# Products of constants in the waits of TensorE, in a twelve-sublayer decoder on one core

## The reference, cut to what matters

```python
x = _layernorm(x + sublayer(x, ...), axis=-1)
```

```python
logits = jnp.einsum('bqhd,bkhd->bhqk', q, k) * scale
w = jax.nn.softmax(logits, axis=-1)
attn = jnp.einsum('bhqk,bkhd->bqhd', w, v).reshape(b, n, H * HD)
return attn @ Wout + bout
```

## Time and profile before

| | us |
|---|---|
| median of three timed executions | 1999.76 |
| the profiled execution, its own time | 2003.11 |
| its span from first to last instruction | 2001.3 |
| TensorE matmul busy | 1604.5 (80%) |
| VectorE busy | 1437.1 (72%) |
| TensorE weight load busy | 1193.9 (60%) |
| ScalarE busy | 777.8 (39%) |
| GpSimd busy | 522.6 (26%) |
| mean granted TensorE clock | 0.870 of full |

### The profile page before, as it was taken

The page is one execution under the profiler, slowest core; times in us unless marked ns, Lnnn a source line. Parts: engine busy times, 40 slices in busy tenths (PEclk is TensorE's granted clock), DMA queues, the critical chain, the costliest instruction groups (busy, mean ns, idle before and its releaser), DMA issues. The chain is left out here.

```text
span 2001.3 us, 31707 instructions
## 1 busy us (share of the span) xinstructions
PE 1604.5 (80%) x11439; PEld 1193.9 (60%) x11470; DVE 1437.1 (72%) x2398; ACT 777.8 (39%) x1231; POOL 522.6 (26%) x588
## 2 busy tenths in 40 slices
PE   4899999999868987266748568899995997888863
PEld 4678888887854663022446434588774885645631
DVE  3299999998645844899578573556774995657698
ACT  2367777675231532233324321433342002425532
POOL 1233333332412401377213002310000330414200
PEclk8999999999977986587878768999996998798985
DMA  3000000000000000000100001000001220010000
GB/s 143 23 28 29 26 26 26 26 26 1 1 11 13 2 7 34 0 0 0 45 3 2 27 37 72 2 25 11 12 21 42 74 73 27 4 56 2 2 0 21
DMA packets 17854, 49.20 MB, mean 25 GB/s; under 512 B 2003, under 2 KB 8276, under 8 KB 16470
## 3 DMA queue, kind: packets, MB, share of 16 engines
q1 hardware_dynamic: 17750, 47.78, 7.0%
HBM read 46.73 MB, written 1.05 MB: 24 GB/s over the span
## 5 line engine op out<-in xcount | busy, mean ns | idle before, releaser
L2146 DVE SCALAR_TENSOR_TENSOR arena<-psum,arena 128x1016 f32<-128x1016 f32 (+2 forms) x240 | 303.6, 1265 | 35.8 <-ACT arena L2083 30.1
L883 DVE TENSOR_REDUCE limits<-psum 128x4 f32<-128x512 f32 (+2 forms) x256 | 148.3, 620 | 91.9 <-PE psum L743 56.7
L1992 PE MATMUL psum<-ssm_XT_hi,ssm_split 128*128 128x512 f32 x640 | 195.1, 407 | 11.2 <-POOL ssm_split L1951 5.5
L851 ACT ACTIVATE PT<-psum 128x1024 f32<-128x1024 f32 x112 | 108.6, 1022 | 122.2 <-PE psum L774 122.2
L743 PE MATMUL psum<-K,QR 32*128 32x256 f32 (+1 forms) x320 | 125.1, 476 | 27.3 <-POOL K L719 16.5
L1992 PEld LDWEIGHTS psum<-ssm_XT_hi,ssm_split 128*128 128x128 f32 x640 | 116.3, 191 | 36.6 <-POOL ssm_split L1951 10.4
L2083 ACT ACTIVATE arena<-psum,arena 128x1024 f32<-128x1024 f32 x80 | 89.2, 1115 | 106.1 <-PE psum L1992 104.7
L2511 PE MATMUL psum<-expert,x 128*128 128x256 f16 x1024 | 114.2, 276 | 16.6 <-POOL expert L2497 16.6
L2649 POOL TENSOR_TENSOR fed<-dtx,b_all 128x1024 f32<-128x1024 f32 x32 | 103.2, 3245 | 77.8 <-ACT b_all L2698 44.4
L2511 PEld LDWEIGHTS psum<-expert,x 128*128 128x128 f16 x1024 | 101.3, 99 | 29.4 <-issue 16.7
L2524 DVE SCALAR_TENSOR_TENSOR acc<-psum,gate_now,acc 128x256 f32<-128x256 f32 x256 | 111.2, 483 | 8.5 <-PE psum L2511 7.7
(11 more groups left out here) (435 smaller groups left out, 3828.4 us busy)
## 6 DMA issues: line engine op xcount, KB each, us to landing
expert_mask<-in_expert_masks SPq DMA_DIRECT2D x32, 256.0 KB, 2.6
arena<-in_ssm_in SPq DMA_DIRECT2D x16, 384.0 KB, 2.9
arena<-in_L_xattn SPq DMA_DIRECT2D x1, 5120.0 KB, 16.0
arena<-in_ssm_in SPq DMA_DIRECT2D x16, 256.0 KB, 3.0
arena<-in_L_ffn SPq DMA_DIRECT2D x1, 2592.0 KB, 10.1
arena<-in_L_xattn SPq DMA_DIRECT2D x2, 1280.0 KB, 7.8
arena<-in_L_attn SPq DMA_DIRECT2D x1, 2272.0 KB
arena<-in_L_ffn SPq DMA_DIRECT2D x1, 2176.0 KB, 8.2
```

The costliest lines, as they stand in the source:

```text
L851: nc.scalar.activation(PT[:, u % 2, 2 * k:2 * k + 2, :, :].rearrange("p r h q -> p (r h q)"), p.psum[:, (2 + 2 * k) * 512:(4 + 2 * k) * 51 ...
L883: ins = nc.vector.tensor_reduce(limits[:, u % 2, r, :, k], score_bank(r)[:, :].rearrange("p (h k) -> p h k", h=4)[:, :, lo:hi], AX.X, ALU. ...
L1992: ins = nc.tensor.matmul(bank[tile_bank(r, tile) + half][:, :], w_part(tile, kw, c), x_part(kx, c, slice(half * 512, (half + 1) * 512)), s ...
L2146: ins = nc.vector.scalar_tensor_tensor(out[:, :, ago:], product[:, :, :P - ago], tap, out[:, :, ago:], ALU.mult, ALU.add)
```

## The change

A helper issues a number of products of the two constants, 128 x 512 each, with no wait before them and no reader behind them. In `attend` it is called ahead of scores 0 and 2 of the first unit and behind score 3 (6, 4 and 7 products, into bank 7). In `epilogue`, where there is no product, it is called ahead of each `turn_x` (6, 3, 3 and 2 products, into bank 0).

```diff
+def hold_clock(p, bank, times):
+
+    for _ in range(times):
+        p.nc.tensor.matmul(bank[:, :], p.c16("ident"), p.c16("after_row"), start=True, stop=True)
...
             def turn_x(j):
+                if added is None:
+                    hold_clock(p, bank[0], (6, 3, 3, 2)[j])
                 for b, ready in ((2 * j, s.x_ready), (2 * j + 1, s.x_odd_ready)):
                     pe.wait_ge(ready.sem, ready.at(j))
...
             for r in range(4):
+                if r % 2 == 0:
+                    hold_clock(p, bank[7], (6, 0, 4)[r])
                 score(0, r)
+            hold_clock(p, bank[7], 7)
             pe.wait_ge(s.loaded.sem, s.loaded.at(15))
             for u in range(U + 2):
```

## The result

The changed kernel took 1972.68 us (median of 4, 1971.30 to 1974.68) against 2000.80 for the kernel before beside it: ratio 0.9859, 95% interval 0.9842 to 0.9876, about 28 us faster. I had forecast 1986 in a range of 1975 to 1998. The direction held, and so did the clock as its cause. The size did not: the saving is twice the forecast, near rival (c), in which the clock holds through heads and ends and to which I had given 0.11.

The account below looks back on a forecast made before the run. The prediction took latency to bound the kernel: TensorE waits at sublayer ends and attention heads, then runs at half clock. Heads 6.1 + ends 8.0 = 14.1 us, so 1999.8 - 14.1 = 1985.7, say 1986 us, range 1975 to 1998.

Parts of the forecast that it names:

- rival (c): Heads and ends: the clock holds through both, 31.2 us saved, hence 1969 us, 1965 to 1977; chance 0.11.
- The prices: Each added 128x512 product costs 0.216 us at full clock, 0.427 at half; all 155 cost 33 or 66 us.
- the fit: Attention heads at full clock: 6 products take 1.3 of 1.8 us, 4 take 0.86 of 0.92, 7 take 1.5 over 1.39.
- The bounds: Most that could be saved: 18.9 us at the attention heads, 13.2 us at the sublayer ends.
- with 0.3 to 0.6 us lost: Ends with a low clock: it should rise amid the transposes, well before the next block, at this small loss.
- 8.0 us of 13.2: Five ends together: 0.4, 1.3, 1.5, 2.4 and 2.4 us, 8.0 in all, between -10.5 and 13.2.
- In the light attentions the fall is put off to the first unit, not taken away: Attention heads: nothing is added inside the loop, so the clock falls in the first unit; the first attention saves 0.8 of 5.5 us.
- 6.1 us of 18.9: Five attention heads together: 0.8 - 0.9 + 4.5 + 1.4 + 0.3 = 6.1 us, between -4 and 18.9.
- The second attention: Its head: added products late at half clock, 3.1 us in all; saving -0.9 us, between -3.1 and 0.
- (a): Ends stay at half clock, added products cost 2.1 us per end; 2004.2 us, slower; chance 0.08.
- (b): Ends pay 8.0 us, heads nothing, as the clock falls in the first unit; 1992 us, 1989 to 1996; chance 0.25.
- (d): Gains and delays cancel, or head gains are lost when the clock falls later; 1997 to 2001 us; chance 0.10.

Follow-up runs that it names:

- thin: The changed kernel with all 155 added products 32 columns wide instead of 512, timed beside the kernel before: 1997.75 us, ratio 0.9976.
- double numbers: The changed kernel with every number of added products doubled, timed beside the kernel before: 1995.52 us, ratio 0.9968.
- those between: Against the kernel before, only the 3, 3 and 2 products ahead of the later transposes in each of five ends: 1989.08 us, ratio 0.9931.
- ends: The changed kernel without the added products in `attend`, so only 14 in each of five ends, against the kernel before: 1985.40 us, ratio 0.9918.
- first six: Against the kernel before, only the 6 products ahead of the first transposes in each of five ends: 1995.13 us, ratio 0.9971.

## Why the prediction was wrong

The prices and the fit were right. An added product adds 0.216 us at full clock and 0.427 at half, 6, 4 and 7 fit at full clock, and from one group of transposes to the next it is 0.87 us with two products between and 1.74 with six, as the prices say. The bounds were nearly right: the ends gave 13.7 us in the profile for a bound of 13.2. What failed were the shares that I took of the bounds, in two steps. The first is the larger and the surer.

**"L0_attn, L1_ffn and L2_ffn ... with 0.3 to 0.6 us lost", and 8.0 us of 13.2.** The ends were undersized: 13.7 us in the profile (2.7, 2.1, 2.1, 3.8, 3.0 for 0.4, 1.3, 1.5, 2.4, 2.4), 14.1 in the second, 10.8 in the profile of the ends alone, and 16 us timed with the ends alone. The 5.7 us that were missing had three sources.

- 1.2 us: at L1_ffn and L2_ffn the clock was low and came back by the second or third group, as forecast, but the loss that I took off is given back in full, since the rounds at full clock, 0.44 + 0.65 = 1.09 us by the prices, are shorter than VectorE's (1.51) and catch up.
- 2.3 us: at L0_attn the clock did not fall, though TensorE idled 2.26 us ahead of the block, 1.12 behind the six and 2.49 behind the transposes. My reason for 0.4, the DMA wait behind the end, came true in the profile of the ends alone (0.1 us) and not in the two of the changed kernel.
- 2.2 us: at L1_attn and L2_xattn I had expected a full clock and still took 1.3 and 2.4 of bounds of 2.1 and 3.8. The prediction gives no reason for that, and there was none: they paid 2.1 and 3.8.

**"In the light attentions the fall is put off to the first unit, not taken away", "the later units as before", and 6.1 us of 18.9.** The fall is put off, but how far differs between two executions of the same kernel. In the first profile of the changed kernel the clock falls at 643.2, in the third unit of the first attention, and in the second at 633.6, at the start of the second unit:

```profile
632.50:643.20 10.70, 8.12 (x118) 5.29 (x119) 8.14 (x14) 5.05 (x8) 6.20 (x7) 1.00 0.01 2
643.23:646.64 3.41, 3.41 (x44) 2.31 (x38) 2.21 (x6) 1.94 (x2) 0.00 (x0) 0.50 0.02 5
```

```profile
629.85:633.60 3.75, 2.51 (x29) 1.48 (x29) 2.93 (x6) 1.79 (x3) 1.81 (x2) 1.00 0.00 0
633.64:647.26 13.62, 13.11 (x128) 9.07 (x128) 7.58 (x14) 5.52 (x10) 4.39 (x5) 0.50 0.01 2
```

It is 3.4 us at 0.50 in the one and 13.6 in the other, where the kernel before had 23.9, from 629.6 to 653.5. The other profiles show the same. In the first and fifth attention, of all kernels without products in the loop, six falls that begin in the third unit last 3.4 us each, six in the second 10.2 to 13.7, and two in the first 13.7. All told these two attentions are at 0.50 for 13.7 to 23.9 us in the kernels without the seven (or with thin ones) and for 3.4 to 13.7 in those with them. I had priced a later fall like an earlier one. Why a late one is short is not shown: that TensorE has no pauses at half clock (3.41 busy of 3.41) can't be all of it, since it is busy for 13.11 of 13.62 us in the long one too.

So the sizes scatter. Four first units of the first attention gave 3.9 us in the first profile and 1.3 in the second for a forecast of 0.8, those of the fifth 2.9 and 0.8 for 0.3 (part of which is not the change's, see below), three of the fourth 2.4 and 1.8 for 1.4, two of the third 4.4 in both for 4.5. The first and the fifth in the second profile:

```profile
629.85:651.55 21.70, 1.08 (x4) 0.38 (x4) 0.69 0.01 2
1775.80:1796.90 21.10, 1.00 (x4) 0.35 (x4) 0.68 0.01 2
```

The third, where the argument was from heavy units, was right, though not with unit 0 "nearly all at half clock": it was at 0.50 for 6.8 of its 10.1 us. Timed, the heads alone brought 15 us, 3 more or less, for 6.1; by the profiles, without what is not the change's, it is 10 and 8.5.

**The second attention.** The added products are late there, as forecast, but by less: 1.6 us from the first score to the first turn of limits, from the comparison with the kernel without, where I had 0.8 + 1.6 = 2.4. For the whole +1.2 us in one profile and -0.5 in the other stand against a forecast of +0.9, so the sign stays open, and so does whether leaving it out helps.

**The rivals.** (a), the half clock that costs more than it gives, fails even in the kernel with nothing ahead of the first transposes, where the clock is low at the start of every end. Late products cost more than a few tenths of a microsecond only at double numbers, and there at full clock. (b), heads that pay nothing, is what the six and the four alone do. (c) is nearest in the time: it took the bounds whole. But the clock did not hold through the first units. (d) is ruled out.

The Trainium skill's rule that a transpose does not count for the clock ("TensorE: Matmul & The Clock Gate", "Part 4: PE-mode transpose") would have given rival (a). The earlier trace rows speaks against the rule, and no later run tests it by itself: where the clock rises amid an end, as in the kernel with only those between, half of the work is transposes and half added products.

**One part is not the change's.** The profile of the kernel before has its fifth attention 3 us, and its fourth 1.4 us, longer than three kernels that add nothing there ("ends", "thin", "first six"). Read from one profile, these 4.4 us look like a gain of the heads. The timed heads-only kernel (15 us) does not need them, but a unit's length in a single profile is a draw. The 3.3 us between the first attention and L1_attn are another matter: five kernels without the seven, or with thin ones, have 0.0 to -0.1 there, and eight with them -0.1 to -3.3, the changed kernel's second profile -1.3. So the heads seem to reach into this stretch, which holds no added product; how is not shown. I can't say what sets these draws; the timed medians carry the claims of size, the profiles those of place.

## What to carry to other kernels

Where TensorE waits ahead of dense dependent work, fill the wait with products of constants into an idle bank, sized to end just before the wait does: price them from the kernel's own rows at both clocks, and remember that at twice the number 20 of the 26 us are gone again. Fill the last wait ahead of the dense stage first; filling an earlier one alone was worth nothing at the heads and 6 of 16 us at the ends. When you estimate what a fall of the clock costs, ask where in the loop it begins: here 3.4 us of half clock from the third unit on, 10 to 14 from the first or second, up to 24 from the head. And profile the changed kernel twice before you explain a part of a gain.

## What I had not expected of the hardware

- Pauses of one length do not have one outcome. At L1_ffn transposes with pauses of 0.40 us stayed at 0.50 for 5 us, six products ahead of them or not; with the pauses filled the clock was full by the last group. At L2_ffn, in the kernel with only the first six, the clock came back amid the transposes over such a pause. At L0_attn of the changed kernel, coming from full clock, pauses of 2.26 and 1.12 us did not lower it; at L2_xattn with only the first six, pauses of 1.12, 0.76 and 0.77 did.
- A fall of the clock that begins one unit later can be 10 us shorter: 3.4 us at 0.50 and 13.6, in two executions of one kernel.
- 155 products of 32 columns hold nothing: the ends, and the heads that were at half clock before, are at half clock as if they weren't there.
- Of stages whose code is the same in two kernels several moved by 1 to 5 us, with no instruction changed in them. The 576 us ahead of the first added product, the same in all, differ by up to 3 us from profile to profile.
